# A graph-attention kernel on one core: the gathering engine copies 64 columns, and waits for the copy, ahead of each unit's two gathers

## The reference

```python
xl = (x @ Wl + bl).reshape(n, HEADS, DIM)
xr = (x @ Wr + br).reshape(n, HEADS, DIM)
e = jax.nn.leaky_relu(xl[src] + xr[dst], NEG_SLOPE)
score = jnp.einsum('ehd,hd->eh', e, att)
smax = jax.ops.segment_max(score, dst, num_segments=n)
ex = jnp.exp(score - smax[dst])
denom = jax.ops.segment_sum(ex, dst, num_segments=n)
alpha = ex / (denom[dst] + 1e-16)
msg = xl[src] * alpha[..., None]
out = jax.ops.segment_sum(msg, dst, num_segments=n)
```

## Time and profile before

| | |
|---|---|
| median of 3 runs | 2965.46 us (2965.15 to 2966.74) |
| the profiled execution | 2963.76 us |
| its span in the trace | 2962.2 us |
| PE busy | 2063.1 us, 70% of the span |
| DVE busy | 1642.5 us, 55% |
| POOL busy | 1573.4 us, 53% |
| ACT busy | 1431.7 us, 48% |

### The profile page before, as it was taken

One profiled execution on the slowest core, in us unless ns is written; L12 is line 12 of the kernel. 1 busy time (PEld: TensorE's weight loads), 2 busy tenths in 40 slices (PEclk: granted clock), 3 DMA queues, 4 the chain that ended last, 5 costly groups with the idle time before them and its releaser, 6 DMA issues. The chain is left out here.

```text
span 2962.2 us, 91209 instructions
## 1 busy us (share of the span) xinstructions
PE 2063.1 (70%) x22500; PEld 1274.6 (43%) x22500; DVE 1642.5 (55%) x6669; ACT 1431.7 (48%) x4238; POOL 1573.4 (53%) x1656
## 2 busy tenths in 40 slices
PE   2457787777777777777734677777777777777674
PEld 1134444444444544444422445444444444444452
DVE  6535555655655655655532555555555555555563
ACT  2334555455555555555532354455554554554554
POOL 1656655555555555555305665555555555555540
PEclk6779989999998989989866999979999999999995
DMA  2434444344444444444203444433433434344430
GB/s 71 155 100 120 118 120 120 111 117 115 112 118 112 116 119 112 116 117 114 79 29 103 120 113 114 114 108 107 114 109 111 112 111 110 110 111 111 110 100 8
DMA packets 227405, 317.35 MB, mean 107 GB/s; under 512 B 47889, under 2 KB 157574, under 8 KB 227270
## 3 DMA queue, kind: packets, MB, share of 16 engines
q0 software_dynamic: 75072, 208.30, 26.4%
q1 hardware_dynamic: 152198, 107.47, 12.1%
HBM read 295.61 MB, written 19.99 MB: 107 GB/s over the span
## 5 line engine op out<-in xcount | busy, mean ns | idle before, releaser
L904 POOL DMA_INDIRECT rows<-table,src_t x1564 | 1526.2, 976 | 1126.8 <-PE psum L1026 606.3
L995 PE MATMUL psum<-ident,rows 128*128 128x128 f32 x3128 | 537.8, 299 | 366.9 <-issue 114.9
L1090 ACT COPY wgt<-psum 128x128 f32<-128x128 f32 x782 | 207.6, 265 | 1207.6 <-PE psum L1026 822.6
L1195 DVE SCALAR_TENSOR_TENSOR acc<-acc,keep,psum 128x129 f32 x782 | 272.8, 349 | 807.2 <-PE psum L1026 361.1
L995 PEld LDWEIGHTS psum<-ident,rows 128*128 128x128 f32 x3128 | 366.3, 151 | 536.6 <-issue 535.4
L1095 ACT ACTIVATE lz<-psum 128x512 f32<-128x512 f32 x782 | 471.3, 603 | 117.5 <-remote 68.4
L1026 PE MATMUL psum<-rows,wgt 128*32 128x129 f32 x6256 | 357.3, 301 | 127.2 <-DVE acc L1195 99.5
L1019 PE MATMUL psum<-ident,ex 128*128 128x128 f32 x782 | 261.2, 334 | 157.9 <-ACT wgt L1090 129.0
L1012 PE MATMUL psum<-lz,att_w 128*32 128x128 f32 x6256 | 361.1, 302 | 0.2
L1101 ACT ACTIVATE ex<-hold_s,peak 128x128 f32<-128x128 f32 x782 | 314.4, 402 | 29.9 <-issue 15.8
L998 PE MATMUL psum<-oh,xrw 96*128 96x256 bf16 x1564 | 325.0, 291 | 1.3 <-issue 1.3
(11 more groups left out here) (242 smaller groups left out, 2147.0 us busy)
## 6 DMA issues: line engine op xcount, KB each, us to landing
xrw<-xr_split SPq DMA_DIRECT2D x782, 48.0 KB
relb<-rel_d SPq DMA_DIRECT2D x194, 192.0 KB
rows<-table,src_t POOLq DMA_INDIRECT x1564
xr_split<-split SPq DMA_DIRECT2D x50, 192.0 KB, 1.9
table<-row SPq DMA_DIRECT2D x50, 130.0 KB, 1.9
x_mid<-x SPq DMA_DIRECT2D x25, 64.0 KB
xo<-x_mid SPq DMA_DIRECT2D x25, 64.0 KB
xo<-in_x_dram SPq DMA_DIRECT2D x24, 64.0 KB
```

Source lines behind the costliest of these rows:

```text
L904: pool.indirect_dma_start(rows[:, i % RING, t, :, :].rearrange("p h c -> p (h c)"), None, s["tables"][layer][0:NP, :], bass.IndirectOffset ...
L995: pe.matmul(z[:, o:o + P], rows[:, k, t, h, 0:D], s["ident"][:, :], is_transpose=True, start=(h == 0 and t == 0), stop=False, skip_group_c ...
L1195: v.scalar_tensor_tensor(a, a, s["keep"][:, bass.ds(at(-11), 1)], ps[5][:, 0:D + 1], ALU.mult, ALU.add).then_inc(added, 1)
```

## The change

From the 17th unit of each layer on, POOL waits for `sums_ready` as before, then copies 64 columns of `sel` (a constant of all 128 partitions, fp32) into a tile `pause` that nothing reads, waits until that copy has signalled its completion, and then issues the two gathers. The first 16 units of a layer are gathered as before. Nothing of the result depends on the copy.

```diff
@@ -761,6 +761,7 @@
     gate = sem("gate")
     moved = sem("moved")
     listed = sem("listed")
+    paused = sem("paused")
     xo_in = sem("xo_in")
@@ -828,6 +829,7 @@
     ex = sb("ex", [P, 2, P], F32)
     wgt = sb("wgt", [P, 2, K * HW], F32)
     hop = sb("hop", [1, NU], F32)
+    pause = sb("pause", [P, HW], F32)
     nm, acc = s["nm"], s["acc"]
@@ -899,6 +901,9 @@
             for i in range(NU):
                 if i >= RING:
                     pool.wait_ge(sums_ready, i - RING + 1)
+                    pool.tensor_copy(pause[:, :], s["sel"][:, 0, 0:2, :].rearrange("p c w -> p (c w)")
+                                     ).then_inc(paused, 1)
+                    pool.wait_ge(paused, i - RING + 1)
                 for t in range(K):
                     c = i * K + t
```

## The result

The change costs time. Median 3043.55 us (3041.52 to 3045.73) against 2966.1 us (2965.15 to 2969.03) for the kernel before, measured beside it on the same chip: ratio 1.026, 95% interval 1.0242 to 1.0277. The prediction was 2967.5 us, and no change likelier than slower; the time lies outside its range.

What follows compares the result with a forecast made beforehand. Waits between engines bound it, no engine near full, POOL following PE's pace. Profiled 2963.76 + 0 + 0 + 0 + 2 + 0 = 2965.8 us, runs' median 1.7 above: 2967.5; likeliest case 2960 to 2971, 8 in 10 2953 to 2992.

Steps and rivals of the forecast that it cites:

- Step 3: Gathers after PE's signal: each first gather starts 0.4 to 0.9 us later, against 12 us of lead; cost 0.
- step 2: Gaps around POOL's copy: 0.07 us in front, 0.30 behind; own cycle 2.97 us, under PE's 3.37 us step; cost 0.
- Step 1: The added copies on POOL: 750 x 0.397 = 298 us more POOL time, all within 1.17 us of room a step.
- Step 4: DVE instructions running beside the copy: 149 places where PE waits for DVE, 0.013 us each, 2 us.
- Step 5: DMA: 750 pairs of gathers shift some 0.8 us against `relb` and `xrw`; sign unknown, taken as 0.
- The copy holds DVE: Slower rival: the copy slows DVE's two-input instruction beside it; 24 us with the middle row, 2990 us; chance 0.26.
- POOL becomes the bound: Slower rival: copy and gaps exceed 1.17 us a unit, so POOL sets the pace; 3001 to 3190 us; chance 0.06.
- Faster: Rival: later gathers get out of the way of `relb` and `xrw` transfers; up to 16 us, half gives 2957; chance 0.20.

Runs made afterwards that it cites:

- The late pair without a copy: Kernel before, no copy, POOL's gathers waiting for ACT's `wgt` instead of `sums_ready`: 3090.81 us, 1.0311 on a slow chip; 1.0044 and 1.0054 on quick ones.
- the kernel without gathers: Kernel before with the gathers replaced by two plain loads of fixed rows per unit, issued by ACT: 2565.4 us, 0.8565 (slow chip); 2564.49 us, 0.9953 (quick).
- the one with the names alone: Changed kernel without its copies and waits, only the semaphore and the tile `pause` declared: 2998.09 us, 1.0002 of the kernel before, on a slow chip.

## Why the prediction was wrong

**Step 3, gathers later against 12 us of lead, is the one that failed**, and with it the sentence of step 2 that "what hides it is PE's pace". The lead is real: PE waits for `rows` only at the start of a layer. But the data was not what tied the gathers to the path. PE's pace was itself set by them: the step of about 3.2 us is 0.18 (from ACT's release to the gather) + 2.20 (the pair) + about 0.8 to the next release. The late pair without a copy (1.031) and the kernel without gathers (0.857) show both halves of this. I had costed a moved step by its readers alone, and had taken the idle 0.99 us of POOL for room. The rows that spoke against it were in the trace: ACT idle for 2 us before each L1090, the last 1.0 to 1.5 us of it after L1026 had ended by its record.

*Step 1* overstated the copy, 0.276 us for 0.397, and 207 us for 298 in all. *Step 2* had the gap behind it right (0.27 us for 0.30), and none was found in front: the copy starts 0.02 us before ACT's L1095 (median), a gather in its place 0.18 after. So the first gather starts 0.3 us later, not 0.77. What it missed is that a gather behind a copy and its wait starts late even if the copy ended long ago (0.69 us). *Step 4* had its number right (L1207 287 ns, L1183 286 ns, no wait of PE for `acc` added), but partly by luck: it laid the copy beside the start of L1207 in nearly every unit, and the copy comes so early that it meets 32 of the 782. *Step 5* was right within 12 us: `relb` 153.5 us for 141.6, `xrw` 103.7 for 105.1.

*The rivals.* The copy holds DVE: fell, since one element costs as much as 64 columns, and the late pair as much with no copy at all. The Trainium skill (GPSIMD Engine Reference, Key points) names contention with a DVE instruction that has two SBUF inputs, as L1207 has. This trace hardly tries it: the 32 that meet the copy have a mean of 284 ns, all 782 one of 287, and it was 287 before. POOL becomes the bound: not on the chip of the result, where it idles 532.6 us before the copies; on the quick ones it comes close, with its own cycle of 2.75 us. The gather starts 0.27 us after each copy, so copy and gather don't push each other's code out (the Trainium skill, GPSIMD Engine Reference, Instruction dispatch, has 6 us for such a load; none is seen). Faster: not seen. No rival had the mechanism that decided.

**What the size is made of is only partly known.** The pair ends 0.35 us later after its signal; were that all added, 750 steps would make 262 us, and it was 77. Some steps with node work are longer than the hold anyway (5.6 us at one place of layer 1's cycle before, 5.7 now), and the signals that slip out make short steps. And TensorE's clock: between the kernel before and the one with the names alone, on two slow chips, the cycle of layer 1 took 54.4 us with 14% of the time at the lower level and 55.4 with 23%, some 11 us for the whole of it. By that estimate, from one pair of traces on two chips, the change's rise (18% to 23% in layer 0, 14% to 29% in layer 1) would be 0.5 of the 1.1 us of layer 0 and 1.6 of the 2.4 us of layer 1. Within one trace of a slowed kernel the cycles with more of it are longer in layer 0, by 5 to 16 us for the whole of it (21 cycles in each of five traces); in layer 1 three of the five show nothing (-1 to 1 us) and two 6.5 and 11 us. Two windows of each, the kernel before, then the change:

```profile
1186.40:1296.00 109.60, 84.00 (x916) 51.51 (x916) 64.06 (x266) 57.42 (x173) 62.88 (x65) 0.91 0.42 115
...
2387.20:2496.80 109.60, 78.90 (x915) 49.87 (x916) 61.88 (x251) 55.55 (x166) 62.77 (x65) 0.94 0.40 110
```

```profile
1186.40:1296.00 109.60, 85.48 (x914) 52.52 (x914) 64.13 (x264) 56.45 (x170) 71.94 (x96) 0.92 0.41 114
...
2387.20:2496.80 109.60, 82.80 (x835) 50.30 (x827) 57.39 (x235) 51.63 (x156) 67.80 (x92) 0.86 0.38 105
```

The columns are busy us and counts of PE, PEld, DVE, ACT and POOL, then the clock, the DMA engines' share and GB/s. In layer 0, at 0.92 for 0.91, DVE and ACT got through 264 and 170 instructions for 266 and 173; in layer 1, at 0.86 for 0.94, through 235 and 156 for 251 and 166. Most of the loss lies in layer 1, where the clock fell most. Whether it fell because PE stood idle in the long steps, or made them, no run separates.

## What to carry to other kernels

A producer that is far ahead of its reader is not thereby off the path: look also at what it shares with the engines that seem to set the pace, and when an engine is released a microsecond or two after the last recorded instruction that it could be waiting for, ask what else ends just before each release. To cost a later start, put the moved instruction beside the whole step's signals, not beside the wait for its data. And where a kernel may run on several chips, measure a change of a few per cent on more than one.

## What the hardware did that I had not expected

- On the slow chips PE's completion signals come mostly 0.6 to 1.0 us after POOL's indirect gathers had ended, at the median 1.1 us after the recorded end of L1026 and 2.4 us in one row above; on the quick ones 0.04 us after it (median), gathers or not. ACT's signals are prompt on both. The kernel before takes 16% longer on the slow chips (2999 against 2576 us), and replacing the gathers removes the whole difference (2565.4 us). PE's records meanwhile go on: L995 starts at 2228.70 and L1012 at 2229.59, before ACT is let go at 2229.68. What holds the signals, whether the array is held or only the signal (the records' ends are modelled), and what differs between the chips, stays open, as does which side of the gathers does it (POOL's work, the software queue, the scattered rows).
- A copy of one element on POOL takes 214 ns, one of 128x64 276 ns, and the gather behind it starts 0.27 us after its end.
- A gather whose last predecessor on POOL is a copy with a wait for it starts 0.69 us after ACT's release by the same signal, against 0.18 us behind another gather, though the copy ended 1.2 us before at the median, and 3 us before in the row above.
